# Loading the operands of a Gram matrix from two queues: the transfers of k are issued by POOL, those of q stay with SP

## The chip, the cores and the metric

The kernel runs on 1 core of one Trainium2 chip. Times are device microseconds (us) of one execution. The engines are PE (matrix products), DVE (vector), ACT (activations), POOL (GpSimd) and SP (SyncE, which here only issues transfers). PEld is PE's weight load. SPq and POOLq are the instruction queues from which SP and POOL issue DMA transfers. All transfers, whoever issues them, are carried out by the core's 16 DMA engines.

## The reference, cut to what matters

The whole program is two layers on a 4 x 192 x 128 x 128 fp32 image: an attention over channels with a parallel convolution branch, and a recurrent mixer. The change touches one step of the first layer, the scores between the channels of q and k of each head:

```python
q, k, v = jnp.split(qkv, 3, axis=1)
q = _l2norm(q.reshape(b, heads, cpg, hw))      # heads 4, cpg 48, hw 16384
k = _l2norm(k.reshape(b, heads, cpg, hw))
attn = jnp.einsum('bhcn,bhdn->bhcd', q, k) * temperature
```

The kernel computes the 48 x 48 Gram matrix of the raw q and k of each head, and the sums of squares of all 96 channels beside it, and divides afterwards.

## The kernel before, in words

The program is a row of stages with a barrier between them. The stage before the Gram stage (`depthwise`) leaves q, k and v as one fp32 image per batch in the DRAM tensor `d`; the stage behind it (`branch_conv`) reads `d` again, and already shares its loads between SP and POOL. The Gram stage is `gram_scores` (L557 to L677). Its tensors and semaphores carry the prefix `gr_` in the profile.

It has NI = 16 units of work, one for each batch and head, which are called heads here and counted from 0 to 15. For each, 96 channels (48 of q, then 48 of k) of 128 rows by 128 columns of fp32 are brought into one half of `qk`, with the image's row as the partition: 6 MB for a head. `qk` has two halves, used in turn. A load of a head is 8 transfers (ND = 8, the first four of q, the last four of k) of 12 channels each: 768 KB, cut into 12 x 128 = 1536 runs of 512 bytes (L589). SP issues them all, in order. Before the load of head n it waits for `product` of head n-2 (PE has made the Gram matrix of the head that had this half) and for `squared` of head n-2 (ACT has squared all of it). Both operands of a head count on one semaphore, `loaded`, so nobody sees q before k.

What then happens with a head:

- ACT (L637) squares it in NE = 4 parts of 24 channels, parts 0 and 1 being q and parts 2 and 3 k, into one of two halves of `sq`. Between heads it finishes the head before: two short copies from PE's results (L628, L630).
- DVE (L653) sums each part over the columns into `ss`. After the four parts it scores the head before (L658 to L673, nine short operations, the last of which raises `scored`).
- PE (L614) makes the Gram matrix as 128 products, one for each column, which the trace shows as 256 matmul instructions, into one of two banks `pg`. It may start a head when it is loaded and head n-2 is scored. Then it waits for DVE's four sums and adds them over the partitions (L618).
- POOL makes two small constants at the stage's start and has nothing else to do in it.

The order is fixed: each engine works its own list from the first head to the last, and every link between the lists is a semaphore.

Of the kernel before, what the change touches and what calls it, by code (L numbers as in the profile page):

```python
# [23 lines left out]
B, C, H, W = 4, 192, 128, 128  # L24
HW = H * W
HEADS, CPG = 4, 48
# [11 lines left out]
def wait(engine, sem, value):  # L38

    if isinstance(value, int) and value <= 0:  # L40
        return
    engine.wait_ge(sem, value)
# [503 lines left out]
def image(d, b):  # L546

    return d[b, ROW:ROW + C3 * HW].rearrange("(c t) -> c t", t=HW)


def gram_scores(nc, d, temperature, attn_d):


    QK, NI, E = 2 * CPG, B * HEADS, 24
    NE = QK // E
    with Stage(nc, "gr") as st:
        qk = st.sb("qk", [128, 2, QK, W])  # L557
        sq = st.sb("sq", [128, 2, E, W])
        ss = st.sb("ss", [128, 2, QK])
        ones = st.sb("ones", [128, CPG])  # L560
        ident = st.sb("ident", [CPG, CPG])
        temp = st.sb("temp", [CPG, HEADS])
        gb = st.sb("gb", [CPG, 2, CPG])
        ga = st.sb("ga", [CPG, CPG])
        nrm = st.sb("nrm", [CPG, 2, QK])
        nqd = st.sb("nqd", [CPG, CPG])
        nq = st.sb("nq", [CPG, 1])
        a = st.sb("a", [CPG, NI, CPG])
        pg = [st.ps(f"p{h}", [128, CPG]) for h in range(2)]
        pn = [st.ps(f"n{h}", [CPG, QK]) for h in range(2)]  # L570
        loaded = [st.sem(f"loaded{h}") for h in range(2)]
        consts, vectors, product, normed, squared, reduced, copied, rooted, scored, small, stored = map(
            st.sem, ("consts", "vectors", "product", "normed", "squared", "reduced", "copied", "rooted", "scored", "small",
                     "stored"))
        block = st.block()
        ND = 8

        @block.sync
        def _(sp):
            sp.dma_start(temp[:, :], bass.AP(temperature.tensor, 0, [[0, CPG], [1, HEADS]])).then_inc(vectors, 16)  # L580
            for n in range(NI):
                b, hd = divmod(n, HEADS)
                wait(sp, product, n - 1)
                wait(sp, squared, NE * (n - 1))
                img = image(d, b).rearrange("c (h w) -> h c w", h=H)
                for k in range(2):
                    c0 = k * C + hd * CPG
                    for e in range(0, CPG, 12):
                        sp.dma_start(qk[:, n % 2, k * CPG + e:k * CPG + e + 12, :],  # L589
                                     img[:, c0 + e:c0 + e + 12, :]).then_inc(loaded[n % 2], 16)  # L590
            sp.wait_ge(scored, NI + 2)
            sp.dma_start(attn_d.rearrange("(n c) k -> c n k", c=CPG), a[:, :, :]).then_inc(stored, 16)
            sp.wait_ge(stored, 16)

        @block.gpsimd
        def _(pool):
            nc.gpsimd.memset(ones[:, :], 1.0).then_inc(consts, 1)
            nc.gpsimd.memset(ident[:, :], 0.0).then_inc(consts, 1)
            pool.wait_ge(consts, 2)
            nc.gpsimd.affine_select(out=ident[:, :], in_=ident[:, :], compare_op=ALU.not_equal, fill=1.0,  # L600
                                    base=0, pattern=[[-1, CPG]], channel_multiplier=1).then_inc(consts, 1)

        @block.tensor
        def _(pe):
            pe.wait_ge(consts, 3)
            with pe.Fori(0, B) as b:
                for hd in range(HEADS):
                    h = hd % 2
                    pe.wait_ge(loaded[h], 16 * ND * (2 * b + hd // 2 + 1))
                    pe.wait_ge(scored, HEADS * b + hd + 1)  # L610
                    pe.wait_ge(rooted, HEADS * b + hd + 1)
                    for w in range(W):
                        p = 64 * (w % 2)
                        mm = nc.tensor.matmul(pg[h][p:p + CPG, :], qk[:, h, 0:CPG, w], qk[:, h, CPG:QK, w],  # L614
                                              start=w < 2, stop=w >= W - 2, skip_group_check=True)
                    mm.then_inc(product, 1)
                    pe.wait_ge(reduced, NE * (HEADS * b + hd + 1))
                    nc.tensor.matmul(pn[h][:, :], ones[:, :], ss[:, h, :], start=True, stop=True).then_inc(normed, 1)  # L618

        @block.scalar  # L620
        def _(act):
            act.sem_inc(rooted, 2)

            def finish(n):
                h = n % 2
                act.wait_ge(product, n + 1)
                wait(act, scored, n + 1)
                nc.scalar.activation(gb[:, h, :], pg[h][64:64 + CPG, :], ACT.Copy).then_inc(copied, 1)  # L628
                act.wait_ge(normed, n + 1)
                nc.scalar.activation(nrm[:, h, :], pn[h][:, :], ACT.Sqrt).then_inc(rooted, 1)  # L630

            for n in range(NI):
                h = n % 2
                act.wait_ge(loaded[h], 16 * ND * (n // 2 + 1))
                for e in range(NE):
                    wait(act, reduced, NE * n + e - 1)
                    nc.scalar.activation(sq[:, e % 2, :, :].rearrange("p c w -> p (c w)"),  # L637
                                         qk[:, h, E * e:E * e + E, :].rearrange("p c w -> p (c w)"), ACT.Square).then_inc(squared, 1)
                if n:
                    finish(n - 1)  # L640
            finish(NI - 1)

        @block.vector
        def _(dve):
            dve.sem_inc(scored, 2)
            dve.wait_ge(consts, 3)
            dve.wait_ge(vectors, 16)

            def reduce(n):
                for e in range(NE):  # L650
                    dve.wait_ge(squared, NE * n + e + 1)
                    wait(dve, normed, n - 1)
                    nc.vector.tensor_reduce(ss[:, n % 2, E * e:E * e + E], sq[:, e % 2, :, :], AX.X, ALU.add).then_inc(reduced, 1)  # L653

            def score(n):
                h, hd = n % 2, n % HEADS
                dve.wait_ge(rooted, n + 3)
                nc.vector.tensor_scalar(nrm[:, h, :], nrm[:, h, :], 1e-12, None, ALU.max).then_inc(small, 1)  # L658
                dve.wait_ge(product, n + 1)
                nc.vector.tensor_copy(ga[:, :], pg[h][0:CPG, :]).then_inc(small, 1)  # L660
                dve.wait_ge(small, 8 * n + 2)
                nc.vector.tensor_tensor(nqd[:, :], nrm[:, h, 0:CPG], ident[:, :], ALU.mult).then_inc(small, 1)
                nc.vector.reciprocal(nrm[:, h, CPG:QK], nrm[:, h, CPG:QK]).then_inc(small, 1)
                dve.wait_ge(small, 8 * n + 4)
                nc.vector.tensor_reduce(nq[:, :], nqd[:, :], AX.X, ALU.add).then_inc(small, 1)
                dve.wait_ge(copied, n + 1)
                nc.vector.tensor_tensor(ga[:, :], ga[:, :], gb[:, h, :], ALU.add).then_inc(small, 1)
                dve.wait_ge(small, 8 * n + 6)
                nc.vector.reciprocal(nq[:, :], nq[:, :]).then_inc(small, 1)
                dve.wait_ge(small, 8 * n + 7)  # L670
                nc.vector.scalar_tensor_tensor(a[:, n, :], ga[:, :], nq[:, 0:1], nrm[:, h, CPG:QK], ALU.mult, ALU.mult).then_inc(small, 1)
                dve.wait_ge(small, 8 * n + 8)
                nc.vector.tensor_scalar(a[:, n, :], a[:, n, :], temp[:, hd:hd + 1], None, ALU.mult).then_inc(scored, 1)  # L673

            for n in range(NI):
                reduce(n)
                if n:  # L677
                    score(n - 1)
            score(NI - 1)
# [1127 lines left out]
def build(nc, io, out):  # L1807
# [20 lines left out]
    pointwise(nc, x, stat0, io["w1t"], io["gate_b1"], io["gate_w2t"], io["gate_b2"], u, gate_sums)  # L1828
    depthwise(nc, u, io["qkv_dw_w"], io["turned_w"], d)
    gram_scores(nc, d, io["temperature"], attn_d)  # L1830
    branch_conv(nc, d, io["fcb"], io["branch_w"], io["branch_b"], attn_d, rank_d, t)
    attention_weights(nc, attn_d, rank_d, gate_sums, io["projt"], pt_d)
# [54 lines left out]
```

## Time and profile before

| | |
|---|---|
| median of 3 runs | 7589.34 us (7576.14 to 7606.34) |
| profiled execution, its own time | 7605.69 us |
| span of the profiled execution | 7603.8 us |
| Gram stage in it | from 2586.9 us to 3051.6 us, 465 us, 6.1% of the span |

Busy time is not waiting time: an engine can be busy for longer than its work needs. A DMA row of the profile tells how long the issuing engine was held by the instruction; the landing time (issue to the last byte) stands apart. POOL's spans are rough. The count of DMA packets in a queue, together with the bytes, tells in which pieces the DMA engines handle that queue's transfers.

### The profile page before, as it was taken

How to read it: one execution, taken by the hardware profiler on the slowest of the kernel's cores; microseconds unless marked ns; L12 is line 12 of the kernel's file. 1: busy time of each engine (PE TensorE's matmuls, PEld its weight loads, DVE VectorE, ACT ScalarE, POOL GpSimd, SP SyncE). 2: the span in 40 equal slices, each digit the busy share in tenths (PEclk: the TensorE clock that was granted, in tenths of full speed). 3: DMA queues.
4: the chain of work that ended last, by engine and by line, in shares of the span. 5: the costliest groups of instructions: out<-in, count | busy, mean ns of one | idle time of the engine just before them, and what ended most of it. 6: DMA issues, size and time to landing. Idle time of an engine off the chain costs nothing. (4 is left out here: it accounts for less than half of the span.)

```text
span 7603.8 us, 83182 instructions
## 1 busy us (share of the span) xinstructions
PE 5831.6 (77%) x25278; PEld 2314.8 (30%) x25278; DVE 5756.3 (76%) x5546; ACT 2658.7 (35%) x3511; POOL 675.1 (9%) x731
## 2 busy tenths in 40 slices
PE   0999999599899567456655777688578879976887
PEld 0333333244333367233332222222122223222222
DVE  6333332499999788787885666599899978997998
ACT  0222222111111378111110000055477764546777
POOL 0000010000000000222220000000022210002221
PEclk9999999799999878677877787789788888777888
DMA  7455555699999997799997999744366644445664
GB/s 293 151 179 167 165 178 169 160 276 276 272 275 274 238 233 200 182 250 249 250 249 183 262 268 264 195 180 185 149 213 217 223 152 174 182 166 189 220 222 167
DMA packets 1209067, 1615.60 MB, mean 212 GB/s; under 512 B 87605, under 2 KB 907510, under 8 KB 1195510
## 3 DMA queue, kind: packets, MB, share of 16 engines
q1 hardware_dynamic: 1067125, 1419.06, 63.6%
q10 hardware_dynamic: 115200, 100.71, 5.2%
q0 software_dynamic: 26624, 94.40, 5.0%
q8 instruction: 58, 0.95, 0.1%
q14 instruction: 60, 0.48, 0.0%
HBM read 1006.55 MB, written 607.33 MB: 212 GB/s over the span
## 5 line engine op out<-in xcount | busy, mean ns | idle before, releaser
L496 PE MATMUL dw_p<-dw_it,dw_tt 128*128 128x512 f32 x2304 | 1025.5, 606 | 177.0 <-DMA dw_it<-u 127.7
L536 DVE SCALAR_TENSOR_TENSOR dw_vo<-dw_vi,dw_wv,dw_vo 128x2048 f32<-128x2048 f32 x384 | 903.1, 2352 | 13.6
L831 PE MATMUL bc_p<-bc_z,bc_wc 128*32 128x256 f32 x9216 | 569.8, 413 | 402.1 <-DVE bc_z L870 402.1
L870 DVE STREAM_TRANSPOSE bc_z<-bc_xp 128x1536 f32<-128x1536 f32 x256 | 711.0, 2843 | 155.6 <-DMA bc_xp<-d 154.9
L339 DVE COPY pw_ut<-pw_p 112x512 f32<-112x512 f32 x384 | 247.4, 686 | 692.7 <-PE pw_p L291 692.7
L1079 PE MATMUL ap_p<-ap_vt,ap_pw 96*96 96x512 f32 x1024 | 586.7, 739 | 188.3 <-DMA ap_xt<-in_x 181.5
L496 PEld LDWEIGHTS dw_p<-dw_it,dw_tt 128*128 128x128 f32 x2304 | 442.5, 194 | 760.1 <-issue 731.8
L288 PE MATMUL pw_p<-pw_xh,pw_wlo 128*112 128x512 f32 x768 | 428.3, 639 | 183.9 <-POOL pw_xh L263 183.9
L511 ACT ACTIVATE dw_ot<-dw_p 128x512 f32<-128x512 f32 x384 | 207.1, 607 | 995.3 <-DMA d<-dw_ot 685.8
L831 PEld LDWEIGHTS bc_p<-bc_z,bc_wc 128*32 128x32 f32 x9216 | 320.9, 119 | 651.0 <-issue 486.6
L809 ACT ACTIVATE bc_xt<-bc_p 128x256 f32<-128x256 f32 x384 | 147.5, 384 | 874.5 <-PE bc_p L831 874.5
L1710 POOL TENSOR_SCALAR wf_bvf<-wf_bvl,wf_fac 128x512 f32<-128x512 f32 x192 | 334.0, 1752 | 1057.0 <-ACT wf_fac L1643 1057.0
L291 PE MATMUL pw_p<-pw_xh,pw_whi 64*112 64x512 f32 x768 | 426.5, 636 | 0.0
L290 PE MATMUL pw_p<-pw_xh,pw_whi 64*112 64x512 f32 x768 | 426.4, 635 | 0.0
L653 DVE TENSOR_REDUCE gr_ss<-gr_sq 128x24 f32<-128x3072 f32 x64 | 344.6, 5470 | 104.1 <-ACT gr_sq L637 103.3
L289 PE MATMUL pw_p<-pw_xh,pw_wlo 128*112 128x512 f32 x768 | 393.2, 594 | 0.0
L1112 DVE TENSOR_TENSOR ap_xo<-ap_p,ap_tt 96x512 f32<-96x512 f32 x256 | 172.3, 685 | 287.9 <-PE ap_p L1079 166.8
L637 ACT ACTIVATE gr_sq<-gr_qk 128x3072 f32<-128x3072 f32 x64 | 340.6, 5396 | 141.7 <-DMA gr_qk<-d 107.5
L614 PE MATMUL gr_p<-gr_qk 128*48 128x48 f32 x4096 | 297.1, 342 | 112.6 <-DMA gr_qk<-d 77.6
L1079 PEld LDWEIGHTS ap_p<-ap_vt,ap_pw 96*96 96x96 f32 x1024 | 201.8, 203 | 573.0 <-issue 534.1
L316 ACT ACTIVATE pw_ut<-pw_p 112x512 f32<-112x512 f32 x256 | 138.7, 594 | 604.5 <-PE pw_p L291 604.5
L614 PEld LDWEIGHTS gr_p<-gr_qk 128*48 128x48 f32 x4096 | 295.0, 244 | 117.0 <-issue 106.4
(314 smaller groups left out, 10164.9 us busy)
## 6 DMA issues: line engine op xcount, KB each, us to landing
u<-pw_ut SPq DMA_DIRECT2D x64, 2240.0 KB, 12.6
dw_it<-u SPq DMA_DIRECT2D x192, 512.0 KB, 7.1
d<-dw_ot SPq DMA_DIRECT2D x192, 512.0 KB, 7.5
gr_qk<-d SPq DMA_DIRECT2D x128, 768.0 KB, 9.1
bc_xp<-d SPq DMA_DIRECT2D x256, 288.0 KB, 12.2
bc_xp<-d POOLq DMA_DIRECT2D x256, 288.0 KB, 9.9
gs_xt<-in_x SPq DMA_DIRECT2D x24, 2048.0 KB, 7.3
d<-dw_vo SPq DMA_DIRECT2D x96, 512.0 KB, 7.8
```

The lines of the kernel that those rows point to most:

```text
L288: mm(pa[:, :], wlo[:, wm], xh[:, h, 0, cols], start=True, stop=False, skip_group_check=True)
L289: mm(pb[:, :], wlo[:, wm], xh[:, h, 2, cols], start=True, stop=False, skip_group_check=True)
L290: mm(pa[:, :], whi[0:64, wm], xh[0:64, h, 1, cols], start=False, stop=True, skip_group_check=True)
L291: mm(pb[:, :], whi[64:128, wm], xh[64:128, h, 1, cols], start=False, stop=True, skip_group_check=True).then_inc(product, 1)
L496: mm = nc.tensor.matmul(po[c][:, :].rearrange("p (b w) -> p b w", b=B), tt[:, h, 3 * c + dx, 0:H], it[:, h, B * c:B * (c + 1), dx:dx + W], ...
L536: nc.vector.scalar_tensor_tensor(vo[:, h], src, w, vo[:, h], ALU.mult, ALU.add).then_inc(tapped, 1)
L614: mm = nc.tensor.matmul(pg[h][p:p + CPG, :], qk[:, h, 0:CPG, w], qk[:, h, CPG:QK, w], start=w < 2, stop=w >= W - 2, skip_group_check=True)
L637: nc.scalar.activation(sq[:, e % 2, :, :].rearrange("p c w -> p (c w)"), qk[:, h, E * e:E * e + E, :].rearrange("p c w -> p (c w)"), ACT.S ...
L653: nc.vector.tensor_reduce(ss[:, n % 2, E * e:E * e + E], sq[:, e % 2, :, :], AX.X, ALU.add).then_inc(reduced, 1)
L831: mm = nc.tensor.matmul(po[q % NBANK][32 * c4:32 * c4 + 32, :, :], wc[:, c, dx, :, :].rearrange("p j r -> p (j r)"), z[:, h, c, :, dx:dx + ...
L870: last = nc.vector.transpose(z[:, h, :, b % 2, 1 + S * k:1 + S * k + S], xp[:, b % 2, k, :, :].rearrange("p s c -> p c s"))
L1079: mm = nc.tensor.matmul(po[2 * q + m][:, :], pw[:, b, k, m * HALF:(m + 1) * HALF], vt[:, b % 2, k, q * SUB:(q + 1) * SUB], start=k == 0, s ...
```

## The change

The loop that issued all 8 transfers of a head from SP becomes a function `loads(queue, k, sems)`, called twice: SP calls it for q (k = 0) with the old semaphores `loaded`, POOL calls it for k (k = 1), after its constants, with two new semaphores `k_loaded`. Each call waits for the same two conditions as before. A head's load is now four transfers on each queue, so ND is 4. PE waits for both semaphores before a head. ACT waits for `loaded` before part 0 and for `k_loaded` before part 2. Sizes, shapes and the number of transfers stay as they are.

```diff
-        ND = 8
+        ND = 4
+
+        def loads(queue, k, sems):
+            for n in range(NI):
+                b, hd = divmod(n, HEADS)
+                wait(queue, product, n - 1)
+                wait(queue, squared, NE * (n - 1))
+                img = image(d, b).rearrange("c (h w) -> h c w", h=H)
+                c0 = k * C + hd * CPG
+                for e in range(0, CPG, 12):
+                    queue.dma_start(qk[:, n % 2, k * CPG + e:k * CPG + e + 12, :],
+                                    img[:, c0 + e:c0 + e + 12, :]).then_inc(sems[n % 2], 16)
...
+            loads(sp, 0, loaded)
...
+            loads(pool, 1, k_loaded)
...
                     pe.wait_ge(loaded[h], 16 * ND * (2 * b + hd // 2 + 1))
+                    pe.wait_ge(k_loaded[h], 16 * ND * (2 * b + hd // 2 + 1))
...
                 for e in range(NE):
+                    if e == NE // 2:
+                        act.wait_ge(k_loaded[h], 16 * ND * (n // 2 + 1))
```

What stands in a row on POOL in the Gram stage, before (a semaphore is written under the name of the first stage that used its number, so the names in "waits" are not those of the source):

```order
L595 UNCONDITIONAL_BRANCH [waits barrier_Pool_Activation_PE_DVE_SP_gather]
L597 MEMSET gr_ones 128x48
L598 MEMSET gr_ident 48x48
L600 AFFINE_SELECT gr_ident<-gr_ident 48x48 [waits gs_reduced]
L61 UNCONDITIONAL_BRANCH
```

and after:

```order
L600 MEMSET gr_ones 128x48
L601 MEMSET gr_ident 48x48
L603 AFFINE_SELECT gr_ident<-gr_ident 48x48 [waits gs_rooted]
L587 DMA gr_qk<-d 128x12x128 x8
L587 DMA gr_qk<-d 128x12x128 [waits pw_normed,gs_stored]
L587 DMA gr_qk<-d 128x12x128 x3
L587 DMA gr_qk<-d 128x12x128 [waits pw_normed,gs_stored]
L587 DMA gr_qk<-d 128x12x128 x3
```

The pair of the last two rows repeats for heads 2 to 15. POOL's 64 transfers stand behind its constants, 8 of them without a wait (heads 0 and 1).

On SP at the same place, before:

```order
L580 DMA gr_temp<-in_temperature 48x4
L589 DMA gr_qk<-d 128x12x128 x16
L589 DMA gr_qk<-d 128x12x128 [waits gs_stored,gs_rooted]
L589 DMA gr_qk<-d 128x12x128 x7
L589 DMA gr_qk<-d 128x12x128 [waits gs_stored,gs_rooted]
```

and after:

```order
L592 DMA gr_temp<-in_temperature 48x4
L587 DMA gr_qk<-d 128x12x128 x8
L587 DMA gr_qk<-d 128x12x128 [waits pw_normed,gs_stored]
L587 DMA gr_qk<-d 128x12x128 x3
L587 DMA gr_qk<-d 128x12x128 [waits pw_normed,gs_stored]
```

SP keeps its place and its waits; each head has 4 transfers there in place of 8.

## Rows read from the trace of the kernel before

**Rows 1.** Groups by line, whole Gram stage: count | busy us, mean ns | idle before, releasers

```profile
L653 DVE TENSOR_REDUCE gr_ss<-gr_sq 128x24 f32<-128x3072 f32 x64 | 344.6, 5470 | 104.1 <-ACT gr_sq L637 103.3
L637 ACT ACTIVATE gr_sq<-gr_qk 128x3072 f32<-128x3072 f32 x64 | 340.6, 5396 | 141.7 <-DMA gr_qk<-d 107.5 <-DVE gr_ss L653 33.6
L614 PE MATMUL gr_p<-gr_qk 128*48 128x48 f32 x4096 | 297.1, 342 | 112.6 <-DMA gr_qk<-d 77.6 <-issue 28.3 <-DVE gr_a L673 6.8
```

**Rows 2.** Busy time by windows: from:to, length, PE, PEld, DVE, ACT, POOL, clock, DMA, GB/s

```profile
2587.00:3052.00 465.00, 303.37 (x4128) 297.78 (x4128) 373.15 (x208) 350.28 (x97) 0.07 (x1) 0.79 0.87 218
```

**Rows 3.** The tile gr_qk: transfers' hold time ns min/median/max, and landing times

```profile
L589 SPq DMA_DIRECT2D gr_qk<-d x128: 367/2640/4431, 2586.9 to 3007.9; - x128
...
DMA to landing us min/median/max: 5.0/9.1/10.9
```

**Rows 4.** Waits in the Gram stage: who <- for whom: us in total, times, longest

```profile
ACT gr_sq L637 <- DMA gr_qk<-d: 107.5, 8, 58.7
DVE gr_ss L653 <- ACT gr_sq L637: 103.3, 9, 48.7
PE gr_p L614 <- DMA gr_qk<-d: 77.6, 4, 59.5
```

**Rows 5.** What SP's queue waited for in the Gram stage: us in total, times, longest

```profile
SPq L42 <- ACT gr_sq L637: 71.5, 10, 12.5
SPq L589 <- PE gr_p L614: 39.7, 3, 16.1
```

**Rows 6.** Timeline around heads 5 to 7: start us, length us, what [idle before]

```profile
2743.28 9.02 ACT L637 ACTIVATE gr_sq<-gr_qk 128x3072 f32<-128x3072 f32 x2 [6.75 <-DMA gr_qk<-d]
...
2749.00 64.33 SPq L589 DMA_DIRECT2D gr_qk<-d  x23
...
2764.32 0.17 PEld L618 LDWEIGHTS gr_n<-gr_ss,gr_ones 128*48 128x48 f32 x2
...
2774.12 20.07 ACT L637 ACTIVATE gr_sq<-gr_qk 128x3072 f32<-128x3072 f32 x3 [12.96 <-DMA gr_qk<-d]
...
2774.33 18.33 PE L614 MATMUL gr_p<-gr_qk 128*48 128x48 f32 x256 [9.64 <-DMA gr_qk<-d]
2784.77 16.28 DVE L653 TENSOR_REDUCE gr_ss<-gr_sq 128x24 f32<-128x3072 f32 x4 [18.58 <-ACT gr_sq L637]
...
2803.01 9.35 PE L614 MATMUL gr_p<-gr_qk 128*48 128x48 f32 x115 [1.36 <-DVE gr_a L673]
```

**Rows 7.** Timeline, ACT alone, where heads 10 and 14 begin

```profile
2887.46 12.61 ACT L637 ACTIVATE gr_sq<-gr_qk 128x3072 f32<-128x3072 f32 x2 [9.62 <-DMA gr_qk<-d]
...
2995.59 21.55 ACT L637 ACTIVATE gr_sq<-gr_qk 128x3072 f32<-128x3072 f32 x2 [5.50 <-DMA gr_qk<-d]
```

**Rows 8.** The tile bc_xp, next stage: hold time of SP's and POOL's transfers, ns

```profile
L730 SPq DMA_DIRECT2D bc_xp<-d x384: 312/317/1661, 3059.9 to 4024.9; - x192
L730 POOL DMA_DIRECT2D bc_xp<-d x384: 550/550/731, 3068.5 to 4026.1; - x192
```

**Rows 9.** Timeline, POOL alone: its first two groups of transfers in the program

```profile
3068.46 6.71 POOL L730 DMA_DIRECT2D bc_xp<-d  x12 [0.43 <-POOL bc_mask L795]
3117.74 3.26 POOL L730 DMA_DIRECT2D bc_xp<-d  x6 [42.57 <-DVE bc_z L870]
```

**Rows 10.** DMA queues 3068 to 3075.4, then 3117.7 to 3120.1: packets, MB, engines' share

```profile
q1 hardware_dynamic: 851, 1.45, 104.3%
...
q1 hardware_dynamic: 190, 0.40, 64.7%
```

**Rows 11.** DMA queues, 3132 to 3140 (both), then 3080 to 3090 (q0 alone)

```profile
q0 software_dynamic: 382, 1.39, 68.5%
q1 hardware_dynamic: 467, 0.67, 36.7%
...
q0 software_dynamic: 551, 1.97, 103.5%
```

**Rows 12.** DMA queues in the Gram stage, 2750 to 2770 us

```profile
q1 hardware_dynamic: 11186, 5.67, 111.3%
```

More of the change, by code:

```diff
@@ L571, in gram_scores @@
         loaded = [st.sem(f"loaded{h}") for h in range(2)]
+        k_loaded = [st.sem(f"k_loaded{h}") for h in range(2)]
         consts, vectors, product, normed, squared, reduced, copied, rooted, scored, small, stored = map(
@@ L580, in _ @@
             sp.dma_start(temp[:, :], bass.AP(temperature.tensor, 0, [[0, CPG], [1, HEADS]])).then_inc(vectors, 16)
[L581 to L590, printed above, removed]
+            loads(sp, 0, loaded)
             sp.wait_ge(scored, NI + 2)
```

## The prediction, made before the changed kernel was run

> **What bounds the kernel now.** I read the stage's groups by line first, then its windows, then who waits for whom, then one stretch of the timeline. The Gram stage is 465 us for 16 heads, 29.0 us a head; nothing else in the program is touched. Three things are each near that. DVE is busy for 373 us of it [rows 2], 344.6 us in the sums alone, ACT squares for 340.6 us [rows 1], and the transfers take 343 us: once the queue is full, SP is held 2.64 us by each of its 128 transfers, about 2.68 us from one to the next [rows 3], which is 768 KB / 2.68 us = 293 GB/s and 21.5 us a head. That hold is the DMA engines' pace and not the price of issuing: the shortest hold is 0.37 us [rows 3], and in 2750 to 2770 the engines are full [rows 12]. So the reader should see that SP's issue is no bottleneck, and that halving its list frees no time.
>
> Where the load ends last is seen in the waits. ACT waits 107.5 us for q and k, 58.7 us of it before head 0, which leaves 48.8 us in 7 waits; PE waits 77.6 us, 59.5 us of it before head 0 [rows 4]. SP in turn waits 71.5 us for ACT's squares (the L42 row is the wait helper) and 39.7 us for PE [rows 5], so it is a loop: a half of the tensor comes free, the load takes 25 us, PE and ACT use it, the half comes free. Rows 6 show one such place. SP starts head 6 at 2749.0, ACT begins it at 2774.1 after 12.96 us of idling, DVE has idled 18.58 us when it gets the first part, and PE 9.64 us. Heads 10 and 14 do the same, ACT idling 9.62 and 5.50 us [rows 7]. Between these places the engines' own chain is last: head 7 starts on PE 1.36 us after DVE scored head 5, though its data was there. So some 6 to 10 us of load time per head can be added or taken at most heads without effect, and at heads 0, 6, 10 and 14 nearly every us counts.
>
> **The change part by part.**
>
> SP loses 64 of 128 transfers. Worth 0: the data still has to pass the same engines at 293 GB/s. PE gets 16 more waits and ACT 16, tens of ns each and done long before in most heads: under 1 us. POOL's waits hold up nobody, since nothing but its own loads is queued behind them, and it is busy 0.07 us in the stage [rows 2].
>
> POOL gains 64 transfers of 1536 runs each. This price t decides the case and no row has it. The nearest rows are the next stage's: POOL is held 550 ns by a transfer of 128 runs, where SP is held 317 ns [rows 8], and 12 of them follow each other in 6.71 us [rows 9]. If 550 ns is mostly a fixed price, t is 0.55 us; if it is all per run, t is 12 x 0.55 = 6.6 us. I take 3.5 us, about the middle. A looser bound from the other side: POOL's queue alone moved 1.97 MB in 10 us [rows 11], 855 runs of 2304 bytes or 11.7 ns a run, 18 us for 1536; but the engines were full there, so that was not POOL's doing, and I leave 18 us as a remote end.
>
> Then the start. The first bytes of POOL's queue came late: issued at 3068.46, none had moved by 3075.4; issued at 3117.74, none by 3120.1 [rows 9, 10]. So 7 us the first time in the program and 2.4 us once warm. This is covered: SP's half of a head alone is 4 x 2.68 = 10.7 us of work, and the engines carry that meanwhile. If that cover goes (q already there), it costs 2.4 us a head.
>
> So k lands when 4t + 2.4 us have passed, or when the engines are done, whichever is later. The point of indifference is 4t + 2.4 = 21.5, t = 4.8 us. At 3.5 us it is 16.4 us, inside the engines' 21.5 us: no loss.
>
> Next, who goes first. With both queues active in 3132 to 3140, q0 (POOL's) moved 1.39 MB and q1 (SP's) 0.67 MB [rows 11]: q0 comes in pieces of 4608 bytes (its runs are 2304 and 1152 long, so they are bundled), q1 in pieces of 2304, which makes about 300 pieces each. The engines alternate piece by piece. In the Gram stage SP's pieces are 5.67 MB / 11186 = 507 bytes, single runs [rows 12]. If POOL's runs are bundled to 4 KB here too, k gets 8 parts in 9 whenever POOL has descriptors ready, and q the rest. For one head that is harmless, the total is the same 21.5 us. But POOL goes on to the next head as soon as its half is free, and then k of head n+1 overtakes q of head n. At head 0 both halves are free: 9.4 MB (k0, k1, q0) / 293 GB/s = 32 us instead of 21.5, so +10 us. At head 6: SP started at 2749.0, PE was done with head 5 at 2764.3 and the load landed by 2774 [rows 6], so k of head 7 can overtake 15 us in, and pushes the end of q of head 6 back by at most its own 10.7 us; the same at heads 10 and 14. Together up to 4 x 10.7 = 43 us, for t below about 3 us. At 3.5 us POOL takes only 768 KB / 3.5 us = 225 of the 293 GB/s, q moves on beside it, and its first bytes are late; I take a third, +15 us.
>
> The Trainium skill, "DMA: Bandwidth & Descriptors", section "Queues, rings and completion order", says that each engine goes round the queues packet by packet, a packet being some 9 to 17 descriptors; the bytes of rows 11 agree with the alternation, though with 2 to 4 runs a packet. By the page's count k would get over 9 parts in 10, which moves no number here.
>
> On the side of gain: bundled pieces may move faster than single runs, and where k is the late one, q lands up to 5 us before it and ACT can square parts 0 and 1 before PE starts. In head 6 three squares took 20.07 us beside PE [rows 6]; early, two would take 2 x 2.8 us and take up to 7 us off the chain, at three heads -21 us. The second needs q ahead, the opposite of the overtaking; I take -7 us for both.
>
> **Sum.** 0 (SP) + 1 (waits) + 0 (POOL's price, hidden) + 15 (order) - 7 (overlap) = +9 us. The profiled execution takes 7605.7 us, 16 us above the median of 7589.3; 7605.7 + 9 = 7615 in its terms, 7598 beside the median, in which the rest is told.
>
> **The rivals.**
>
> *POOL's generation becomes the bound.* For it: each transfer has 12 times the runs of any in POOL's rows. Against it: the 550 ns are the same for the two shapes, and back to back. It decides from t = 4.8 us. At 6.6 us k needs 26.4 + 2.4 = 28.8 us, +7.3 us a head: at the eight heads that wait now 58 us, with some of the others 35 to 95 us, 7625 to 7685. At 9 us POOL alone paces the stage: 16 x 36 + 35 = 611 us, +146 us, 7735. This is the rival on the other side.
>
> *The overtaking in full.* t below 3 us, bundles of 4 KB, and each late head shifting all behind it: three or four of the four places in full, +32 to +43 us, 7621 to 7632.
>
> *The gain.* Shares equal or k slightly behind, faster pieces: -20 to -50 us, 7540 to 7570.
>
> *DVE locks POOL out.* In the first group of rows 9, POOL's first bytes waited 7 us while DVE worked. If DVE's sums kept POOL from writing descriptors, POOL would have 465 - 373 = 92 us for 224 us of generation: about +130 us, 7720. The Trainium skill, "SBUF — State Buffer", section "Who interferes with whom", describes such a lock for DVE copies and tensor-scalar operations in a two-port mode and excludes reductions on this chip, which are nearly all of DVE's time here. I give it little.
>
> **How the numbers follow.** Forecast 0.46; generation bound 0.30; overtaking in full 0.13; gain 0.07; lock 0.04. About 0.5% (38 us) is what a measurement of this kernel can tell from no change. Faster by more: the gain, 0.07. Slower by more: 0.27 of generation, 0.09 of overtaking, 0.04 of the lock, 0.40. The rest, 0.53, is within. Range 7560 to 7690: it leaves out the deep gain (0.04), prices above 7 us and the lock (0.15). The forecast's own range is 7575 to 7627.
>
> **What would show it.** Right: POOL's 64 transfers held under 4.8 us each, the stage between 450 and 495 us, q0's packets near 4 KB, ACT waiting for `loaded` rather than `k_loaded`, head 0 starting a few us later than 24.5 us after SP's first issue. Wrong: POOL busy with transfers without gaps between heads, and PE waiting for k at every head (generation); or ACT's part 0 starting well before PE (gain).

## The result, and the profile after

| | before | after |
|---|---|---|
| median of 12 runs each, same chip | 7593.56 us (7576.14 to 7614.21) | 7641.57 us (7617.21 to 7660.23) |
| ratio after / before | | 1.0056, 95% interval 1.0043 to 1.0069 |
| profiled execution, its own time | 7605.69 us | 7651.48 us |
| Gram stage in it, first issue to last score | 464.7 us | 505.4 us |
| the rest of the span | 7139.1 us | 7143.9 us |

The change costs 43 us by the ratio (33 to 52) and 48 us by the medians. The profiled pair differs by 45.8 us, of which the Gram stage has 40.7. I predicted 7598 us, +9: the time lies inside the range of 7560 to 7690, but beyond the upper end of the forecast's own range, 7627, and beside the rival "the overtaking in full" (+32 to +43 us, 7621 to 7632), whose upper end the ratio just reaches.

The transfers, by the tile `gr_qk` in the profile of after (columns as in [rows 3]):

```profile
L587 SPq DMA_DIRECT2D gr_qk<-d x64: 367/2674/13672, 2585.9 to 3029.6; - x64
L587 POOL DMA_DIRECT2D gr_qk<-d x64: 1015/1017/1656, 2586.4 to 3010.0; - x64
...
DMA to landing us min/median/max: 5.0/14.0/25.0
```

POOL is held 1.017 us by a transfer of 1536 runs, 4.1 us for a head's k, and the engines take 10.7 us for the data. The hold alone does not say when the descriptors are written, but the queue below is not short of them. SP was never held longer than 4.4 us before [rows 3]; now 13.7 us, and the longest landing went from 10.9 to 25.0 us. Something passes SP's transfers.

What passes them stands in the DMA queues. First 2595 to 2605 us, in head 0's load, then 2776 to 2788 us, where k of head 7 has been issued beside q of head 6 (packets, MB, share of the engines):

```profile
q0 software_dynamic: 683, 2.55, 89.2%
q1 hardware_dynamic: 684, 0.35, 15.8%
...
q0 software_dynamic: 710, 2.72, 79.2%
q1 hardware_dynamic: 1559, 0.79, 28.2%
```

In the first stretch the engines take one packet of each queue in turn, 683 to 684. But a packet of q0 (POOL's) is 4096 bytes, eight runs of 512 (all but 16 small ones for each transfer, which are in the count), and one of q1 (SP's) is a single run: k gets 2.55 of 2.90 MB, 88%. The second stretch is less even (SP's packets also move while q0 has no work), and k still gets 77%.

What that does, in the timeline around heads 5 to 7 of after, to be read beside [rows 6]:

```profile
2757.24 98.77 SPq L587 DMA_DIRECT2D gr_qk<-d  x16
2757.51 5.54 POOL L587 DMA_DIRECT2D gr_qk<-d  x4 [31.03 <-PE gr_p L619]
...
2773.52 4.05 POOL L587 DMA_DIRECT2D gr_qk<-d  x4 [10.47 <-PE gr_p L619]
...
2793.55 9.59 ACT L644 ACTIVATE gr_sq<-gr_qk 128x3072 f32<-128x3072 f32 x2 [24.36 <-DMA gr_qk<-d]
...
2793.76 16.00 PE L619 MATMUL gr_p<-gr_qk 128*48 128x48 f32 x256 [20.54 <-DMA gr_qk<-d]
2799.36 14.86 DVE L660 TENSOR_REDUCE gr_ss<-gr_sq 128x24 f32<-128x3072 f32 x4 [24.84 <-ACT gr_sq L644]
```

Head 6 is issued at 2757.24. Its k goes first (2757.51), and at 2773.52 POOL, released by PE, issues k of head 7, which passes what is left of q of head 6. ACT starts at 2793.55, 36.3 us after the issue instead of 25.1. It needs only q for its first part, and PE, which needs both, starts 0.2 us later: q came last. ACT alone at the other three such places (heads 0, 10 and 14; compare [rows 7]):

```profile
2621.40 12.55 ACT L644 ACTIVATE gr_sq<-gr_qk 128x3072 f32<-128x3072 f32 x2 [69.81 <-DMA gr_qk<-d]
...
2910.18 9.05 ACT L644 ACTIVATE gr_sq<-gr_qk 128x3072 f32<-128x3072 f32 x2 [28.25 <-DMA gr_qk<-d]
...
3027.85 20.63 ACT L644 ACTIVATE gr_sq<-gr_qk 128x3072 f32<-128x3072 f32 x2 [28.72 <-DMA gr_qk<-d]
```

| from a head's first issue to ACT's first part, us | head 0 | head 6 | head 10 | head 14 |
|---|---|---|---|---|
| before | 24.5 | 25.1 | 25.2 | 25.4 |
| after | 35.5 | 36.3 | 36.0 | 36.3 |

Four times 10.8 to 11.2 is 44 us. One k is 3.15 MB, and 3.15 MB at the 290 GB/s of the first stretch (2.90 MB in 10 us) is 10.8 us. ACT also waits 8.1 to 8.5 us for q at heads 5, 9 and 13, which makes its 7 waits below, but there PE is still at the head before, so PE has only 4. The waits of the whole stage say it too (answering to [rows 4] and [rows 5]), and the groups (answering to [rows 1]), and the window (answering to [rows 2]):

```profile
ACT gr_sq L644 <- DMA gr_qk<-d: 176.0, 7, 69.8
DVE gr_ss L660 <- ACT gr_sq L644: 168.3, 16, 58.3
PE gr_p L619 <- DMA gr_qk<-d: 133.5, 4, 70.7
```

```profile
L660 DVE TENSOR_REDUCE gr_ss<-gr_sq 128x24 f32<-128x3072 f32 x64 | 318.1, 5039 | 168.5 <-ACT gr_sq L644 168.3
L644 ACT ACTIVATE gr_sq<-gr_qk 128x3072 f32<-128x3072 f32 x64 | 302.3, 4794 | 221.4 <-DMA gr_qk<-d 176.0 <-DVE gr_ss L660 45.2
...
L587 POOL DMA_DIRECT2D gr_qk<-d x64 | 67.7, 1071 | 357.3 <-ACT gr_sq L644 233.2 <-PE gr_p L619 123.7 <-issue 0.4
```

```profile
2586.00:3092.00 506.00, 291.16 (x4128) 286.05 (x4128) 349.33 (x208) 310.60 (x97) 67.69 (x65) 0.75 0.75 200
```

ACT's squares and the idling before them were 340.6 + 141.7 = 482.3 us and are 302.3 + 221.4 = 523.7 us: +41.4, the growth of the stage. 68.5 of it is more waiting for transfers and 11.6 more waiting for DVE; the squares themselves are 38.3 us shorter. POOL is busy for 67.7 us of 506, and waits for ACT and PE, not for itself. The DMA engines' share over the stage fell from 0.87 to 0.75: they carry the same bytes in a longer time. At the four places they are full, and the wrong bytes are first. PE's granted clock is not the cause: it is 0.75 in the stage instead of 0.79, but PE is busy for 291 us instead of 303.

### The profile page after: what moved, and what is told of

It is laid out like the page before. It is cut to its first block and busy times, and to the rows that moved or that the text cites. A ratio compares the mean times of both kernels' runs of the same rounds, so it can differ in the third digit from the quotient of the medians.

```text
span 7649.3 us, 83228 instructions
## 1 busy us (share of the span) xinstructions
PE 5834.0 (76%) x25278; PEld 2298.7 (30%) x25278; DVE 5732.7 (75%) x5546; ACT 2620.8 (34%) x3511; POOL 743.8 (10%) x795
## 5 line engine op out<-in xcount | busy, mean ns | idle before, releaser
L660 DVE TENSOR_REDUCE gr_ss<-gr_sq 128x24 f32<-128x3072 f32 x64 | 318.1, 5039 | 168.5 <-ACT gr_sq L644 168.3
L644 ACT ACTIVATE gr_sq<-gr_qk 128x3072 f32<-128x3072 f32 x64 | 302.3, 4794 | 221.4 <-DMA gr_qk<-d 176.0
```

## The experiments

Profiled executions differ by some 15 us with nothing in the kernel to account for it: the Gram stage of e1 is 452.5 us and that of before 464.7, though the timed comparison has them equal, and the rest of the span goes from 7130 to 7151 us over the profiles. So a verdict on the total goes by the timed comparison, and one on the mechanism by the interval from a head's first issue to ACT's or PE's start, which repeats within about 1 us. Diffs are against after unless said. "Change" is (ratio - 1) times the median of before in the same set (7593.6 us for after; 7603.1, 7599.7 and 7601.4 us for the three sets of experiments).

| kernel | ratio to before, 95% | change, us | ACT starts after issue, heads 0 / 6 / 10 / 14, us |
|---|---|---|---|
| before | 1 | 0 | 24.5 / 25.1 / 25.2 / 25.4 |
| after | 1.0056 (1.0043 to 1.0069) | +43 | 35.5 / 36.3 / 36.0 / 36.3 |
| e1_ordered | 1.0004 (0.9995 to 1.0013) | +3 | 24.1 / 25.4 / 25.6 / 25.2 |
| e11_first_only | 1.0036 (1.0022 to 1.0050) | +27 | 24.3 / 36.4 / 35.9 / 36.3 |
| e4_one_of_eight | 0.9996 (0.9986 to 1.0006) | -3 | 26.8 / 28.2 / 28.7 / 28.0 |
| e10_two_of_eight | 1.0019 (1.0005 to 1.0032) | +14 | 29.7 / 30.9 / 30.7 / 30.8 |
| e8_sp_order | 1.0022 (1.0008 to 1.0035) | +17 | 35.0 / then 25 |
| e7_pool_one_wait | 1.0008 (0.9996 to 1.0021) | +6 | 25.4 / 26.7 / 26.3 / 26.0 |
| e2_all_pool | 0.9959 (0.9945 to 0.9974) | -31 | 14.5 / 15.0 / 15.3 / 21.4 |
| e3_sp_two_sems | 0.9966 (0.9947 to 0.9985) | -26 | 13.5 / 14.4 / 25.1 / 15.1 |
| e6_swap | 1.0028 (1.0014 to 1.0042) | +21 | 20.5 / 24.5 / 20.1 / 19.8 |
| e5_swap_ordered | 0.9975 (0.9964 to 0.9985) | -19 | 20.2 / 18.6 / 20.3 / 18.5 |
| e9_quarters | 0.9942 (0.9919 to 0.9964) | -44 | 7.8 / 8.5 / 8.8 / 8.6 |

In e2 at head 14, in e3 at head 10 and in e6 at head 6 ACT came from other work, idle for less than 0.2 us before it; these three intervals say nothing of the load.

My theory: k of the next head passes q of this one, and that is all of it. Rivals: POOL's queue is slow or late by itself; the extra waits cost; both queues together move less.

**e1_ordered: both queues, but k may not pass.** POOL waits until q of the head before has landed.

```diff
+                if k and n:
+                    queue.wait_ge(loaded[(n - 1) % 2], 16 * ND * ((n - 1) // 2 + 1))
```

> The changed kernel, with one wait more: before the k transfers of head n, POOL waits until q of head n-1 has landed. Theory (overtaking: k of the next head passes q of this head, and each of heads 0, 6, 10 and 14 starts some 11 us later): the overtaking is gone, head 0 starts on PE about 24.5 us after SP's first issue, heads 6, 10, 14 about 25 us after theirs, the Gram stage is 465 +- 8 us, the time that of the kernel before within 10 us. Rival (POOL's queue itself costs, by its late first bytes or by two queues disturbing each other): the stage stays above 490 us and the time 30 to 60 us above the kernel before.

Measured: 1.0004. One wait, which by itself can only delay, takes back all of the 43 us to within the interval (-4 to +10). At head 6 in its timeline:

```profile
2739.45 50.95 SPq L589 DMA_DIRECT2D gr_qk<-d  x12
2739.72 6.30 POOL L589 DMA_DIRECT2D gr_qk<-d  x4 [31.84 <-PE gr_p L621]
...
2764.82 9.60 ACT L646 ACTIVATE gr_sq<-gr_qk 128x3072 f32<-128x3072 f32 x2 [11.06 <-DMA gr_qk<-d]
2765.03 16.08 PE L621 MATMUL gr_p<-gr_qk 128*48 128x48 f32 x256 [7.59 <-DMA gr_qk<-d]
2765.37 5.45 POOL L589 DMA_DIRECT2D gr_qk<-d  x4 [19.36 <-DMA gr_qk<-d]
```

POOL now starts k of head 7 at 2765.37, released by a transfer, right behind ACT's start at 2764.82, which is 25.4 us after the issue. POOL's and PE's extra waits, POOL's generation and the alternation within a head are all still in this kernel, so together they cost nothing that can be measured. The Gram stage of the profile, 452.5 us, is under the 457 to 473 expected, by the spread told above.

**e11_first_only: the same wait, for head 1 alone.**

```diff
+                if k and n == 1:
+                    queue.wait_ge(loaded[0], 16 * ND)
```

> The changed kernel with the added wait for head 1 alone: POOL issues k of head 1 only when q of head 0 has landed; all later heads as in the changed kernel. Theory (overtaking, four places of 11 us each): head 0 starts as before, heads 6, 10 and 14 still 11 us late, so the kernel takes some 11 us less than the changed one, 28 to 38 us over the kernel before. Rival (the loss is one of POOL's first use in the program, at head 0): within 10 us of the kernel before.

Measured: +27 us (17 to 38), just under the 28 to 38 expected, head 0 starting at 24.3 us and the other three at 36. One place of four repaired gives back 16 us (43 - 27, each with an interval of some 10), three places left cost 27: the places add up, at 9 to 16 us apiece.

**e4_one_of_eight and e10_two_of_eight: a smaller dose.** Only the last one, or the last two, of a head's 8 transfers go to POOL (ACT waits for them before part 3). The core of e10; e4 has 7 and `(7,)` in place of 6 and `(6, 7)`:

```diff
-        ND = 4
+        ND = 6
...
+                for part in parts:
+                    k, e = part // 4, part % 4 * 12
+                    sems = k_loaded if part >= 6 else loaded
...
-            loads(sp, 0, loaded)
+            loads(sp, range(6))
...
-            loads(pool, 1, k_loaded)
+            loads(pool, (6, 7))
```

> Only the last of the eight transfers of a head (channels 36 to 47 of k) is issued by POOL, the other seven by SP. Theory (overtaking): what can pass is one transfer of 768 KB, 2.7 us instead of 10.7 at each of the four places, so 8 to 14 us over the kernel before. Rival (a fixed price of having two queues, such as the late first bytes or the new waits): as much as in the changed kernel, 40 to 50 us.

> The last two of the eight transfers of a head (channels 24 to 47 of k) are issued by POOL, the other six by SP; ACT waits as late as before. Theory (overtaking): 1.5 MB can pass, so heads 0, 6, 10 and 14 start 5.4 us later after their issue than before (about 30.5 us), twice the 2.7 us of one transfer and half the 10.7 us of four. Time: 8 to 21 us over the kernel before, the lower end since one transfer on POOL delayed the starts but not the whole.

Measured: the start slips by 2.3 to 3.5 us with one transfer and by 5.2 to 5.8 us with two, against 10.8 to 11.2 with four: about 2.7 us for each transfer that can pass, which is 768 KB at 293 GB/s. That is the mechanism, in proportion. The total follows for two (+14; 4 x 5.5 = 22 would be all of it) and for four (+43 of 44), but not for one: -3 (-11 to +5), where I had expected 8 to 14 and the four delays sum to 11.5. Something takes up the first few us at a place. What it is I did not find.

**e8_sp_order: the overtaking without POOL.** The kernel before, with SP alone, and k0, k1, q0, q1 as the order at the start:

```diff
-                for k in range(2):
-                    c0 = k * C + hd * CPG
+                order = ((1, 0), (1, 1)) if n == 0 else ((0, 0), (0, 1)) if n == 1 else ((0, n), (1, n))
+                for k, m in order:
```

> The kernel before with one thing moved: SP issues k of head 0, k of head 1, q of head 0, q of head 1, in that order; POOL issues nothing. It makes by hand, on SP's one queue and at the first heads only, the order in which the changed kernel's data arrive. Theory (order of arrival): head 0 starts on PE 35 us after the first issue instead of 25, and the kernel takes 8 to 12 us more than before. Rival (it takes a second queue to lose time): within 4 us of the kernel before.

Measured: +17 us (6 to 27), above the 8 to 12 expected, though these lie in the interval. The place itself is as expected (timeline from 2586 us):

```profile
2586.67 39.33 SPq L591 DMA_DIRECT2D gr_qk<-d  x16
2621.70 15.81 ACT L639 ACTIVATE gr_sq<-gr_qk 128x3072 f32<-128x3072 f32 x2 [64.34 <-DMA gr_qk<-d]
```

Head 0 starts 35.0 us after the issue, as in after (35.5), with no POOL, no second queue, no second semaphore and no 4 KB packets. At head 0 it is the order of the bytes that costs, not who issues them.

**e2_all_pool and e7_pool_one_wait: POOL's queue alone.** In e2 POOL issues all 8 transfers of a head in order, q on `loaded` and k on `k_loaded`; e7 is e2 with ACT held until k is there too, as the kernel before has it.

```diff
-            loads(sp, 0, loaded)
...
-            loads(pool, 1, k_loaded)
+            loads(pool)
```

and e7 against e2:

```diff
-                    if e == NE // 2:
+                    if e == 0:
                         act.wait_ge(k_loaded[h], 16 * ND * (n // 2 + 1))
```

> All eight transfers of a head are issued by POOL, q then k, in one queue; SP issues none. Theory (overtaking between two queues): one queue is first in first out, so there is nothing to overtake; left are the late first bytes of POOL's queue, 2.4 us at four heads and 7 us the first time, together 5 to 17 us over the kernel before. Rival (POOL's queue itself costs): twice as much traffic on it as in the changed kernel, so at least the 48 us of the changed kernel.

> All eight transfers issued by POOL, but ACT waits for q and k together before part 0, as in the kernel before. It leaves POOL's queue as the only difference to the kernel before. Theory (POOL's queue costs nothing much by itself, and the gain of the version with all transfers on POOL is ACT's early start): the kernel before within 8 us, some 25 us slower than with the early start. Rival (POOL's bundled pieces are the gain): 20 us or more under the kernel before.

Measured: e7 1.0008, the kernel before with POOL in SP's place: not to be told from it (-3 to +16 us), its starts 0.7 to 1.6 us later. So POOL's price and its packets together are worth nothing that shows here. e2 is 31 us faster than before where I had expected it slower: the expectation overlooked that splitting the semaphore lets ACT begin q while k still comes. The pair e2 and e7, one line apart, puts that at 37 us (-31 against +6, each with an interval of some 10).

**e3_sp_two_sems: the same early start, SP alone.** It is e2 with `loads(sp)` in place of `loads(pool)`.

```diff
-            loads(sp, 0, loaded)
+            loads(sp)
...
-            loads(pool, 1, k_loaded)
```

> All eight transfers of a head are issued by SP as before, but q and k count on semaphores of their own and ACT squares the q parts as soon as q is there, as the changed kernel allows. It is the change without POOL. Theory: ACT takes parts 0 and 1 before PE starts at heads 0, 6, 10 and 14, at 2.8 us each instead of 5 to 10, which takes 5 to 7 us off the chain at three or four heads: 15 to 28 us under the kernel before. Rival (PE's chain is last there, ACT's is not): no difference within 5 us.

Measured: -26 us (-40 to -11), within what was expected. One such place in its timeline:

```profile
2765.94 5.58 ACT L644 ACTIVATE gr_sq<-gr_qk 128x3072 f32<-128x3072 f32 x2 [4.24 <-DMA gr_qk<-d]
...
2768.91 6.61 DVE L660 TENSOR_REDUCE gr_ss<-gr_sq 128x24 f32<-128x3072 f32 x2 [2.00 <-ACT gr_sq L644]
...
2777.04 6.30 PE L619 MATMUL gr_p<-gr_qk 128*48 128x48 f32 x77 [10.05 <-DMA gr_qk<-d]
```

ACT squares both parts of q (5.58 us) and DVE sums them before PE starts at 2777.04, 11 us after ACT.

**e6_swap and e5_swap_ordered: q on the fast queue.** POOL issues q and SP k; e5 adds a wait of POOL for k of the head before, e6 has none.

```diff
-            loads(sp, 0, loaded)
+            loads(sp, 1, k_loaded)
...
-            loads(pool, 1, k_loaded)
+            loads(pool, 0, loaded)
```

and in e5 besides:

```diff
+                if not k and n:
+                    queue.wait_ge(k_loaded[(n - 1) % 2], 16 * ND * ((n - 1) // 2 + 1))
```

> POOL issues q and SP issues k, without any added wait: the changed kernel with the roles exchanged. Theory (overtaking): q of the next head passes k of this one, so PE still starts heads 0, 6, 10 and 14 some 11 us late (35 to 36 us after the issue), but ACT has its q parts early. 44 us of delay less some 20 to 28 us of ACT's gain: 10 to 30 us over the kernel before. Rival (ACT's start is what counts, not PE's): no slower than the kernel before.

> POOL issues q and SP issues k, and before q of head n POOL waits until k of head n-1 has landed, so that nothing of the next head can pass. POOL's queue takes most of the engines, so q of a head comes first and ACT can begin with it. Theory (the order of arrival is all that counts): as with all transfers in one queue and ACT starting on q alone, 20 to 35 us under the kernel before, ACT starting heads 0, 6, 10 and 14 some 14 us after their issue and PE 25 us. Rival (two queues disturb each other): no gain over the kernel before.

Measured: e6 +21 us (11 to 32), as expected, but not at the places expected. Now it is k that is passed, and PE waits for it five times:

```profile
PE gr_p L619 <- DMA gr_qk<-d: 150.1, 5, 64.6
```

These are heads 0, 2, 4, 10 and 14: PE starts 35.7, 36.7, 36.7, 36.6 and 36.6 us after the issue, while ACT has q at 19 to 21. Head 6, where k was to be passed too, is not one of them, and heads 2 and 4 are new. So with five delays the kernel loses half of what after loses with four; the early squares are what can give that back. With the order kept (e5), PE starts at 24.7 to 27.0 and the kernel is 19 us faster than before, less than the 20 to 35 expected: ACT gets q at 18 to 20 us, not at 14, because POOL's first bytes come late beside a running SP (3.7 to 5.5 us at these heads, last section), while SP's k takes the engines.

**e9_quarters: one semaphore for each of ACT's four parts, SP alone.** The version that the others point to; the edit is against before.

```diff
+        part_loaded = [[st.sem(f"loaded{part}{h}") for h in range(2)] for part in range(NE)]
...
+                for part in range(NE):
+                    for e in range(E * part, E * part + E, 12):
+                        c0 = e // CPG * C + hd * CPG + e % CPG
+                        queue.dma_start(qk[:, n % 2, e:e + 12, :],
+                                        img[:, c0:c0 + 12, :]).then_inc(part_loaded[part][n % 2], 16)
...
                 for e in range(NE):
+                    act.wait_ge(part_loaded[e][h], 16 * ND * (n // 2 + 1))
```

> SP issues all eight transfers, and each quarter of a head (24 channels, what ACT squares at once) counts on a semaphore of its own, so ACT may begin after two transfers. Theory (ACT's early start is the gain): part 0 can begin 8 us after the issue instead of 14, but DVE and the wait for PE stay, so a little more than with halves: 20 to 35 us under the kernel before. Rival (the gain is used up once q is squared before PE starts): the same as with halves, 18 to 26 us under it.

Measured: 0.9942, 44 us faster than before (27 to 62), the fastest of all. The middle is above the 20 to 35 expected, the interval reaches into it. Its timeline where head 6 begins:

```profile
2731.86 29.47 SPq L587 DMA_DIRECT2D gr_qk<-d  x12
...
2740.37 3.60 ACT L641 ACTIVATE gr_sq<-gr_qk 128x3072 f32<-128x3072 f32 x1 [3.58 <-DMA gr_qk<-d]
...
2746.37 2.79 ACT L641 ACTIVATE gr_sq<-gr_qk 128x3072 f32<-128x3072 f32 x1 [2.39 <-DMA gr_qk<-d]
...
2751.81 2.76 ACT L641 ACTIVATE gr_sq<-gr_qk 128x3072 f32<-128x3072 f32 x1 [2.65 <-DMA gr_qk<-d]
...
2757.23 10.93 ACT L641 ACTIVATE gr_sq<-gr_qk 128x3072 f32<-128x3072 f32 x1 [2.66 <-DMA gr_qk<-d]
2757.55 2.77 PE L618 MATMUL gr_p<-gr_qk 128*48 128x48 f32 x31 [10.56 <-DMA gr_qk<-d]
```

ACT follows the transfers part by part, the first three squares 2.8 to 3.6 us long; the fourth, beside PE, takes 10.93 us. Only one part is left when PE starts, where before all four were.

**e12_few_products: what makes the squares long.** The kernel before, with only 4 of the 128 products of a head; its Gram matrix is left incomplete.

```diff
-                    for w in range(W):
+                    for w in (0, 1, W - 2, W - 1):
```

> The kernel before with most of PE's work in the Gram stage left out: of the 128 products of a head only the first two and the last two are made, so its scores are not those of the reference. Transfers, squares and sums are unchanged. Question: who makes ACT's squares take 5 to 15 us and DVE's sums 5 to 14 us, where both take 2.8 and 3.3 us at other times. If it is PE's reading: all 64 squares take 2.8 us and all 64 sums 3.3 to 3.4 us, and the stage is paced by the transfers, 21.5 us a head, 370 to 400 us. If it is the transfers: the squares and sums stay at a mean of over 4.5 us.

Measured, in one profiled execution: 7501.85 us beside 7623.55 us of before, and in the groups of the Gram stage (columns as in [rows 1]):

```profile
L653 DVE TENSOR_REDUCE gr_ss<-gr_sq 128x24 f32<-128x3072 f32 x64 | 210.1, 3345 | 144.6 <-ACT gr_sq L637 144.6
L637 ACT ACTIVATE gr_sq<-gr_qk 128x3072 f32<-128x3072 f32 x64 | 182.1, 2873 | 203.0 <-DMA gr_qk<-d 182.4 <-DVE gr_ss L653 20.5
```

and its window (columns as in [rows 2]):

```profile
2587.00:2957.00 370.00, 22.53 (x160) 15.31 (x160) 238.16 (x208) 190.62 (x97) 0.00 (x0) 0.50 1.11 272
```

The same squares take 2.87 us instead of 5.40 [rows 1] and the same sums 3.35 instead of 5.47, though the DMA engines are busier than before (272 GB/s, 218 in [rows 2]). So it is PE's products that stretch them, not the transfers. This explains why an early start of ACT is worth so much: a square ahead of PE costs 2.8 us. With PE's work gone the transfers pace every head, ACT idling 8.5 us before each; how much of the 6 to 10 us by which the other engines are behind the transfers in before comes from the stretched squares, and how much from PE's own time, this run does not separate.

## Why the prediction was right or wrong

- **What bounds the stage: held.** Four places (heads 0, 6, 10, 14) where the load is last, all others covered. After shows the same four, each 11 us later; e1 and e11 show that these four make the time.
- **SP relieved: 0. Held**, by e1, which has the relief and gains nothing.
- **Waits: +1.** Too small to be told; e1 has them and more, at +3 (-4 to +10).
- **POOL's price t = 3.5 us: wrong in size.** By the hold it is 1.02 us, near the lower end of 0.55 to 6.6. The middle was taken between "all fixed" and "all per run". From 0.550 us for 128 runs [rows 8] and 1.017 for 1536, a run costs 0.33 ns and the rest, 0.51 us, is fixed: the fixed end was nearly true. The term itself, 0, held: in e7, with all eight transfers on POOL, the load is 0.7 to 1.6 us later and the total the same.
- **Late first bytes: covered, as predicted.** They take 3.7 to 5.7 us and not the 2.4 said (last section); e5 is where they show.
- **The overtaking, +15: this is the step that failed, by its size.** Each part of the mechanism held: alternation packet by packet, POOL's runs bundled to 4 KB, k of head n+1 passing q of head n at heads 0, 6, 10 and 14, 10.7 us each, and the condition t below 3 us. I took a third because at t = 3.5 POOL would have fed only 225 of 293 GB/s. With t at 1.0 k took nearly all of it: 4 x 11 = 44 us, and the measured change is 43. So the wrong t cost nothing in its own term and 29 us in this one; with the 7 us of the gain that makes the distance from +9. That q would also "move on beside it" is right for an eighth of the bytes (0.35 of 2.90 MB) and helps nobody, as a head waits for its last byte.
- **Gain, -7: did not come.** It needed k late and q early; in after PE begins 0.2 us behind ACT at all four places (2793.76 and 2793.55 at head 6), so q was the last. Nor are bundled pieces faster: POOL's queue alone moved 5.22 MB in 18 us in e2 (2592 to 2610), 290 GB/s, and SP's alone 5.80 MB in 20 us in before (2592 to 2612), the same. The two halves of this term and the overtaking exclude each other, as the text said of the second, and still both were summed. Without the term the forecast would have been +16; with the overtaking full, +44.
- **Rivals.** Generation as the bound: out, POOL is held 1.017 us, not 4.8, and its queue alone keeps the engines full (e2). DVE locking POOL out: out, the longest hold is 1.66 us beside DVE's sums, and e7, with all transfers on POOL beside the same sums, is no slower. What was to be seen if right: POOL below 4.8 us, packets near 4 KB and ACT waiting for q came true; the stage was to be 450 to 495 us and is 505; head 0 was to be "a few us" late and is 11.
- **The range.** That the range holds 7641 is luck: it reached to 7690 for a slow POOL, which did not come. And 38 us as the least that can be told was too much: the interval of after is 10 us to either side.

What I should have done: the bounds of t lay on both sides of 3 us, the point where the larger term switches from a part to the whole. A value in the middle of a price's range is no middle of the time when another term depends on it. And a third had no row behind it, while 10.7 us and four places had.

The Trainium skill, "DMA: Bandwidth & Descriptors", section "Issuing engines are not separate DMA queues", says that transfers from any engine interleave on the same 16 engines, and that issuing from several saves only the time of issuing. The first half is what the queues show. The second is too little here: the split changed which bytes come first, and that cost 0.56%. The Trainium skill, "DMA: Bandwidth & Descriptors", section "Queues, rings and completion order", gives packets of about 9 to 17 descriptors; here they hold one run on SP's queue and eight on POOL's, and this inequality decides who is passed.

## What to carry to other kernels

When a load is split over two queues, ask which bytes the consumer waits for last and whether the other queue may issue the next buffer before they are in: with two free buffers it can pass them by a whole half load, and a wait for the slower half (e1) is enough against it. Look at the bytes per packet of each queue before trusting that they share evenly. The gain in this stage was in neither queue but in the semaphores: letting a consumer start on the part that has landed (e3, e9) was worth 26 to 44 us, above all where it then runs clear of the engine that slows it.

## What the runs showed of the hardware

- **POOL's hold hardly grows with the runs.** 1.017 us for 1536 runs, 0.550 us for 128: twelve times the runs, not twice the time. What is written after the hold ends keeps up too: POOL's queue alone moved 290 GB/s (e2), 2.7 us a transfer.
- **POOL's first bytes are late when SP's queue is running, not when POOL is cold.** In after, head 0's k was issued at 2586.4 and nothing of q0 had moved by 2592, while q1 had moved 1.30 MB. In e2, where POOL is alone and its first transfer of the stage goes out at 2586.1, q0 had moved 0.16 MB by 2589. From 2586.4 to 2592 in after and from 2586 to 2589 in e2 (DMA queues):

```profile
q1 hardware_dynamic: 2618, 1.30, 87.4%
```

```profile
q0 software_dynamic: 39, 0.16, 33.5%
```

  Nearly the same stretch of time at the start of the same load, and the same queue: the first row lacks q0 altogether. From POOL's issue to its first packet, read from the traces at every head where no earlier transfer of POOL was outstanding, it is 3.7 to 5.7 us in after and 1.7 to 2.8 us in e2 and e7, first head included (1.9 us in both). Nor was the 2.4 us of [rows 9, 10] the value once warm: later groups of the same stage in before, issued at 3173.60, 3204.55 and 3233.80 into an empty q0 with two other queues running, had their first packet after 5.2, 4.0 and 6.2 us.
- **PE's products slow ACT and DVE.** Products that read columns 512 bytes apart in `qk` stretch ACT's squares of the same tensor from 2.87 to 5.40 us and DVE's sums of another tensor from 3.35 to 5.47 us in the mean (e12). The Trainium skill, "SBUF — State Buffer", section "Who interferes with whom", says that only the port pair shared by DVE and GpSimd causes contention, and that PE and ACT never wait on anyone. These means speak against it: POOL is busy for 0.07 us of the stage in before and 0.00 in e12. By which path they meet, the runs do not say.
- **A hold is not a price.** SP's median hold of 2.64 to 2.67 us is the same with 64 transfers as with 128, and its longest grew from 4.4 to 13.7 us with nothing changed in the transfers themselves; the shortest, 0.367 us, is the same in both. The hold follows what the engines are doing, not the work of issuing.
